# Flamingo block, two layers: steps of the query preparation moved and split in the second cross attention, output projections on the two PSUM banks in the other order

## What is computed

```
x = x + tanh(g_xattn[0]) * xattn0(layernorm(x), ctx)
x = x + tanh(g_ffn[0])   * ffn0(layernorm(x))
x = x + tanh(g_xattn[1]) * xattn1(layernorm(x), ctx, ctx)
x = x + tanh(g_ffn[1])   * ffn1(layernorm(x))
```

```
q = rms_norm(q, q_norm_w); k = rms_norm(k, k_norm_w)      # q from x, k and v from ctx
q = q.reshape(B, T, 16, 32); k, v = k.reshape(B, T, 4, 32), v.reshape(B, T, 4, 32)
q = q * cos + rotate_half(q) * sin;  k = k * cos + rotate_half(k) * sin
scores = (q . k) / sqrt(32), masked above the diagonal
attn = softmax(scores); out = attn . v                    # 4 query heads share one key head
return out @ w_out.T
```

## Time and profile before

| | |
|---|---|
| median of three runs | 845.38 us (844.04 to 846.34) |
| the profiled execution, own time | 847.61 us |
| its span, first to last instruction | 845.8 us |
| mean granted TensorE clock | 0.92 of full speed |
| PE busy | 665.4 us, 79% |
| DVE busy | 644.0 us, 76% |
| ACT busy | 610.5 us, 72% |
| POOL busy | 387.3 us, 46% |
| the stage xattn1, about | 341 to 685 us of the span |

### The profile page before, as it was taken

How to read it: one execution, slowest core, us unless ns; L and a number is a source line. 1 busy time by engine, 2 the same in 40 slices (tenths; PEclk the granted TensorE clock), 3 DMA queues, 4 the chain that set the end, 5 groups by cost and what they waited for, 6 DMA issues and landing times. The chain is left out here.

```text
span 845.8 us, 13637 instructions
## 1 busy us (share of the span) xinstructions
PE 665.4 (79%) x5141; PEld 363.1 (43%) x5174; DVE 644.0 (76%) x978; ACT 610.5 (72%) x814; POOL 387.3 (46%) x493
## 2 busy tenths in 40 slices
PE   8852466885876756769989897989999887888886
PEld 6431123332433323445654564456545533444443
DVE  3689999999999896886894589556634547888884
ACT  3787699898878993588883697479927227777775
POOL 1116535657695774372472156212203416565552
PEclk9976589798989979679999999999999899999999
DMA  8900400000000000622321021122200000100011
GB/s 311 376 5 0 145 4 2 1 0 1 1 0 2 1 0 8 218 69 70 126 74 35 2 70 35 47 70 76 76 1 2 2 34 1 37 27 26 26 38 50
DMA packets 21905, 43.72 MB, mean 52 GB/s; under 512 B 3920, under 2 KB 8528, under 8 KB 21072
## 3 DMA queue, kind: packets, MB, share of 16 engines
q1 hardware_dynamic: 21840, 42.85, 14.8%
HBM read 38.61 MB, written 4.19 MB: 51 GB/s over the span
## 5 line engine op out<-in xcount | busy, mean ns | idle before, releaser
L1660 DVE TENSOR_REDUCE c_nmax<-c_s 128x1 f32<-128x384 f32 (+3 forms) x176 | 108.8, 634 | 83.7 <-PE c_s L1878 83.6
L1778 ACT ACTIVATE c_probs<-c_e 128x512 f32<-128x512 f32 (+1 forms) x176 | 94.5, 558 | 57.1 <-PE c_e L1908 56.0
L1590 POOL TENSOR_TENSOR c_psum<-c_probs 128x1536 f32<-128x1536 f32 x16 | 55.9, 3495 | 155.9 <-ACT c_probs L1778 155.9
L1361 PE MATMUL b_y<-w2q,b_q2T 128*128 128x512 bf16 x254 | 74.2, 445 | 48.8 <-ACT b_q2T L1278 28.7
L2214 PE MATMUL d_gu<-gateq,d_xqT 128*128 128x512 bf16 (+1 forms) x382 | 83.4, 362 | 18.2 <-ACT d_xqT L2139 15.8
L1875 PE MATMUL c_s<-c_kT,c_qaT 96*128 96x128 f16 (+3 forms) x256 | 73.4, 320 | 21.8 <-DVE c_nmax L1660 19.5
L1332 PE MATMUL b_up<-shared,b_xqT 128*128 128x512 bf16 x242 | 70.2, 411 | 3.6 <-ACT hidden L1244 2.5
L1906 PE MATMUL c_e<-c_qaT,c_kT 98*128 98x512 f16 (+3 forms) x256 | 69.8, 307 | 3.6 <-ACT c_qaT L1765 3.6
L1361 PEld LDWEIGHTS b_y<-w2q,b_q2T 128*128 128x128 bf16 x256 | 26.3, 109 | 87.5 <-issue 45.3
L2214 PEld LDWEIGHTS d_gu<-gateq,d_xqT 128*128 128x128 bf16 x384 | 34.9, 98 | 53.2 <-ACT d_xqT L2139 22.7
L1875 PEld LDWEIGHTS c_s<-c_kT,c_qaT 96*128 96x128 f16 x256 | 25.6, 101 | 67.7 <-DVE c_nmax L1660 39.0
(11 more groups left out here) (242 smaller groups left out, 1867.6 us busy)
## 6 DMA issues: line engine op xcount, KB each, us to landing
c_stage<-in_gateT SPq DMA_DIRECT2D x16, 704.0 KB, 4.0
c_stage<-in_downT SPq DMA_DIRECT2D x6, 768.0 KB, 4.4
xs<-in_x SPq DMA_DIRECT2D x4, 1024.0 KB, 15.2
a_w1f<-in_w1T SPq DMA_DIRECT2D x2, 2048.0 KB, 17.2
hidden<-in_w2T SPq DMA_DIRECT2D x2, 2048.0 KB, 21.8
out<-xs SPq DMA_DIRECT2D x16, 256.0 KB, 2.0
b_ln_g<-in_ln_g SPq DMA_DIRECT2D x1, 1024.0 KB, 5.1
b_ln_b<-in_ln_b SPq DMA_DIRECT2D x1, 1024.0 KB, 7.3
```

The source lines that it names most:

```text
L1361: last = nc.tensor.matmul(y_ps[:], q2T[:, n % 2, c, :], w2q[:, c, :], start=(c == 0), stop=(c == IC - 1))
L1590: nc.gpsimd.tensor_tensor(psum[:], region(slot, 0)[:, :, P:], region(slot, 1), ALU.add).then_inc(psum_ready, 1)
L1660: nc.vector.tensor_reduce(nmax[:, G % 2, i, n:n + heads], s_ps[u % 2][:, 0:heads * (i + 1) * P].rearrange("p (n k) -> p n k", n=heads), ax ...
L1778: nc.scalar.activation(probs[:, G % 2, at:at + width], e_ps[fill % 3][:, 0:width], ACT.Exp).then_inc(e_read, 1)
```

## The change

Three things are done.

1. The steps of the preparation of a batch move within the 44 units. `weighted` and `turn_queries` of the four query tiles move from units 16, 18, 20, 22 to 16, 20, 26, 28. `query_heads` on ACT moves from 19, 21, 23, 25 to 20, 24, 29, 31. `query_parts` on DVE moves from 20, 22, 24, 26 to 21, 27, 30, 32. `keys_squared` moves from unit 2 to 3, the keys' scale on POOL from 2 to 4, `keys_scaled` from 5 to 6.
2. Three methods of `Preparation` are split in two. Both halves are called one after the other wherever the whole was called, so this alone moves nothing.
3. The four projections of a batch use the banks tr, y, tr, y instead of y, tr, y, tr.

```diff
+    def keys_variance(self, dve, b):
+        nc = self.nc
+        dve.wait_ge(self.step, self.small.value())
         last = self.small.mark(nc.vector.tensor_reduce(self.kss[:], self.ksq[:], axis=AX, op=ALU.add))
...
+    def key_rest(self, dve, b):
...
+    def weighted_cos(self, dve, b, i):
+        nc, n = self.nc, b * TILES + i
         dve.wait_ge(self.xw_ready, n + 1)
         if n >= TILES:
             dve.wait_ge(self.qlo_ready, n - self.TURNED + 1)
...
-    out_ps = [y_ps[:], den_ps, y_ps[:], den_ps]
+    out_ps = [den_ps, y_ps[:], den_ps, y_ps[:]]
...
-        KEYS, KEYS_SCALED, KEYS_TURNED, KEYS_SPLIT = 2, 5, 8, 18
+        KEYS, KEYS_SCALED, KEYS_TURNED, KEYS_SPLIT = 3, 6, 8, 18
         STATS = 9
-        TURN, EACH, SPLIT = 16, 2, 4
+        WEIGHT_AT = (16, 20, 26, 28)
+        HEADS_AT, PARTS_AT = (20, 24, 29, 31), (21, 27, 30, 32)
...
-                if u == KEYS:
+                if u == KEYS + 1:
                     prep.keys_scale(pool, b)
...
-                    if u == TURN + EACH * i:
+                    if u == WEIGHT_AT[i]:
                         prep.turn_queries(pool, b, i)
...
                 for i in range(TILES):
-                    if u == TURN + EACH * i:
+                    if u == WEIGHT_AT[i]:
                         prep.weighted(dve, b, i)
-                    if u == TURN + EACH * i + SPLIT:
+                        prep.weighted_cos(dve, b, i)
+                    if u == PARTS_AT[i]:
                         prep.query_parts(dve, b, i)
...
-                        if u % SPAN == TURN + EACH * i + SPLIT - 1:
+                        if u % SPAN == HEADS_AT[i]:
                             act.wait_ge(tr_done, TURNS_BEFORE(b))
                             prep.query_heads(act, b, i)
...
-                take(("y", "tr")[i % 2], y_read, b * TILES + i + 1)
+                take(("tr", "y")[i % 2], y_read, b * TILES + i + 1)
```

More of the change, by code:

```diff
@@ L343, in keys_squared @@
             dve.wait_ge(self.khi2_ready, b)
-        last = self.small.mark(nc.vector.tensor_tensor(self.ksq[:], self.kctx[:], self.kctx[:], ALU.mult))
-        dve.wait_ge(self.step, last)
+        self.small.mark(nc.vector.tensor_tensor(self.ksq[:], self.kctx[:], self.kctx[:], ALU.mult))
+    def keys_variance(self, dve, b):
+        nc = self.nc
+        dve.wait_ge(self.step, self.small.value())
         last = self.small.mark(nc.vector.tensor_reduce(self.kss[:], self.ksq[:], axis=AX, op=ALU.add))
@@ L383, in key_parts @@
         self.nc.vector.tensor_copy(ka[:, :, 0:HD], k4).then_inc(self.khi_ready, 1)
+    def key_rest(self, dve, b):
+        k4 = self.ksq[:].rearrange("p t (h j) -> p (t h) j", j=HD)
+        ka = self.kaug[:].rearrange("p t h j -> p (t h) j")
         dve.wait_ge(self.khi_ready, b + 1)
@@ L1144, in _ @@
                     prep.weighted(dve, 0, p - 4)
+                    prep.weighted_cos(dve, 0, p - 4)
                 largest(n + 1)
@@ L1151, in _ @@
                     prep.keys_squared(dve, 0)
+                    prep.keys_variance(dve, 0)
                 if p == 3:
@@ L1159, in _ @@
                     prep.weighted(dve, 0, 3)
+                    prep.weighted_cos(dve, 0, 3)
                 if p == 7:
@@ L1162, in _ @@
                     prep.key_parts(dve, 0)
+                    prep.key_rest(dve, 0)
                     for i in range(TILES):
@@ L1629, in prepare @@
                     prep.keys_squared(dve, b)
+                    prep.keys_variance(dve, b)
                 if u == KEYS_SCALED:
@@ L1638, in prepare @@
                     prep.key_parts(dve, b)
+                    prep.key_rest(dve, b)
                 for i in range(TILES):
-                    if u == TURN + EACH * i:
+                    if u == WEIGHT_AT[i]:
                         prep.weighted(dve, b, i)
-                    if u == TURN + EACH * i + SPLIT:
+                        prep.weighted_cos(dve, b, i)
+                    if u == PARTS_AT[i]:
                         prep.query_parts(dve, b, i)
```

## The result

The changed kernel takes 839.21 us in the median of its runs, the kernel before 845.79 us in the same comparison; the ratio is 0.9925, interval 0.991 to 0.9941. It is thus 6.3 us faster by the ratio and 6.6 by the medians, where 12.9 us were forecast. One of its seven runs took 2213.11 us, is not explained, and is left out of the ratio, which goes by the other six. The profiled execution took 840.96 us, with a span of 839.2 us, 6.6 us less than that of before.

The account below looks back on a forecast made before the run. PE was taken to wait for row maxima behind DVE's work while queries are prepared. Projections 4.5, second preparation 3.2, third 3.7 and first 1.5 sum to 12.9 us: 845.4 to 832.5 us, range 827 to 841.

Parts of the forecast that it names:

- What bounds the kernel: Units 15 to 27: PE waits for row maxima behind DVE's unit 18 work, 5.6, 3.1 and 4.3 us; POOL blocks DVE.
- Projections: Last projection in y: the next group's total no longer waits 1.65 us, three times; 4.5 us gained, 3.0 to 4.95.
- Second preparation: Tiles 2 and 3 leave units 20 to 26 for 26 to 32, under projections: 3.2 us gained, 1 to 4.9.
- First preparation: No projections in units 28 to 31; ACT's idle time can be won: 1.5 us gained, -1.3 to 3.1.
- a sign of being wrong: Units 26 to 33 of the first preparation longer than 11 us, against 10.5 before.
- Third preparation: Tiles 2 and 3 move under the projections, waits and lower clock shrink: 3.7 us gained, 1 to 5.9.
- the stall reappears at unit 20: Low case for second and third preparations, weighted(1) and query_parts(0) following each other: 1 us gained each.
- Keys: L344 one unit later runs free of POOL's sum, 0.8 us of DVE twice; PE doesn't wait there: costed at nothing.
- ACT keeps the pace: Rival, chance 0.2: moved query_heads wait for POOL with exponentials behind; preparation brings some 3.5 us; 837.4 us.
- Only the projections: Rival, chance 0.1: stalls come back whole, at unit 20 and in the first preparation's units 26 to 32; 841.5 us.
- Slower through the clock: Rival, chance 0.04: preparation over more units thins PE's activity; half of 34 us more at 1.2 GHz; 857 us.

Follow-up runs that it names:

- the last experiment: Changed kernel with query_parts of tile 0 in unit 25, but weighted and turn_queries of tile 1 back in unit 18: 833.34 us, ratio 0.9857.
- the sum that waits: Changed kernel, but POOL begins the sum of unit 22 only when query_parts of tile 0 is done: 836.62 us, ratio 0.9877.

## Why the prediction was wrong

**What bounds the kernel.** Right. PE waited for row maxima in unit 21 for the pile of unit 18; the last experiment brings the wait back by one number. That DVE's instruction with two tiles stands still until POOL's ends was right too, and is now shown by the sum that waits: 3.97 against 0.74 us. The Trainium skill's rule ("SBUF — State Buffer", "SBUF: two separate sides") was the right tool; I used it to explain the kernel before and did not carry it through every new place.

**Projections.** Forecast 4.5 us, measured 5.2 in the stage. The wait went three times, and no wait for the first projection's bank took its place.

**Second preparation.** Forecast 3.2 us. The steps alone took 2.4 us off its 44 units, after 0.3 us given back in units 0 to 14 by the key steps. The full clock came back, as the step said; a wait of 1.35 us in unit 21 stayed, and one of 1.45 us in unit 22 was new, behind `query_parts(0)`. With that moved to unit 25 this preparation takes 1.4 us less, so what is missing here comes from the same mistake as in the third.

**First preparation.** Forecast 1.5 us, bounds -1.3 to 3.1; its 44 units lost 3.3 us in one profile and 1.8 in the other. In both, units 28 to 43 grew by 1.3 us (21.2 to 22.5) and units 26 to 33 took 11.1 to 11.2 us instead of 10.5, over the 11 that was named as a sign of being wrong, so the late tiles are not free here; DVE waited 0.8 us for ACT once. What units 15 to 27 gained was more: 3.7 us in one profile, 2.9 in the other. A part of the larger gain, 0.9 us in units 0 to 14, came in one profile and not in the other.

**Third preparation.** This is the step that failed. Forecast 3.7 us less, at the worst 1 us less; the steps alone made its 44 units 1.6 us longer, 5.3 us off, most of the 6.6 us that are missing. (The rest: the stage as a whole lost 8.8 us in one profile and 7.4 in the other, and the times 6.3; of that last difference no step of the sum can be made answerable.) The reasoning named the place, "if the stall reappears at unit 20, where `weighted(1)` and `query_parts(0)` now follow each other", and priced only a wait for maxima. It stated that blocking of about 2 us would go, "because the sum of unit 22 no longer stands behind three turnings". But a sum that comes earlier meets whatever stands in units 21 to 24, and the change had put `query_parts(0)` in unit 21: a collision removed in unit 26 was made in unit 21, of 3.97 us where the old ones were 1.98, 2.70 and 1.95. In unit 26 PE had slack; in unit 21 it had none, and waited 3.89 us, of which the sum that waits gave 3.24 back. With the instruction in unit 25 the third preparation's 44 units take 82.1 us, 4.9 less than before; the banks alone gave 1.7 of that, so some 3.1 us remain for the steps where 3.7 were forecast: the size was nearly right but for this collision. That the long block came in the third preparation alone is likely due to the clip of 1.42 us in unit 20 there, which shifts DVE against POOL, so that L1688 is held by L445 and L459 begins just as POOL's sum does; this was not tried by itself.

**Keys.** Costed at nothing, on the ground that PE doesn't wait there: near enough, but the sign is the other way, for L1701 stands in unit 3.

**The rivals.** "ACT keeps the pace" named 837.4 us, closer to the 839.2 that came, but for the wrong reason: with one instruction of DVE moved, the same ACT gave 831.2. "Only the projections", 841.5 us, was not what happened either, since 4.2 us came from the steps. The right rival, a new meeting of DVE and POOL, was not on the list. The sum of "Slower through the clock" has a slip: the first stretch's busy 17.87 us less half of 10.7 is 12.5, not 16, so the three stretches would be some 27 us longer and not 34, and the rival's time near 854, not 857. The measured time lies within the range; what failed is the size, 6.3 us for 12.9. The forecast of 12.9 us lies between the kernel whose sum waits, 10.4 us, and the one with tile 0 in unit 25, 15.7.

## What to carry to other kernels

When a step is moved away from another engine's long instruction, list that engine's instructions in the new order, with the times that they will then have, and lay every moved step against them: the long one moves too. A blocked instruction costs what the engine that waits for what is behind it can't absorb, so an instruction of 2.70 us in unit 26 left PE without a wait of note, and one of 3.97 us in unit 21 cost it over 3. If the long instruction has slack and the short step has none, one wait that lets the short step go first gives a part back: 3.2 us of the stage here, where the better place gave 6.8.

## What the runs showed of the hardware

The granted clock can add to a stall. A mean of 0.87 over the 27.3 us of the third preparation is 7 us at 1.2 GHz. About half of it lies in the gap of 3.89 us, where PE does nothing and it costs nothing; the rest follows, with a granted clock of 0.50 in the 3.0 us behind the gap (519.24 to 522.24) and 0.96 in the next 3.0. The length of a gap alone didn't say whether this came: the 96x512 matmul took 0.61 us behind 2.73 us of idleness and 0.39 behind 2.93, in one execution. And where it falls is not fixed by the program: the same kernel had 16 matmuls of ffn1 in 5.31 us in one execution and 3.63 in another, and 3.0 us of difference in a part of the program that no edit touched.

POOL is held by DVE as DVE is by POOL. In the second preparation of the changed kernel L445 ends at 432.92, L459 at 433.48, and the sum, started at 432.88, takes 3.89 us, not the 3.42 to 3.46 of most. With the sum made to wait, it took 3.43 in the same place. The changed kernel's line:

```profile
432.88 3.89 POOL L1605 TENSOR_TENSOR c_psum<-c_probs 128x1536 f32<-128x1536 f32 x1
```
